# Pairing the low-rank passes of a fused cross-attention and FFN kernel in 64-row halves, with the group loop written out

## What is computed

```python
# cross-attention: layernorm, q/k/v projections, softmax over 256 keys, output projection
x = x + xattn(layernorm(x), ctx_768, ...)
# FFN with ternary weights and a low-rank term
def bitlinear(x, w):                      # w is rounded to -1, 0, 1 times a scale per row
    scale = clip(mean(abs(w), axis=1, keepdims=True), 1e-05, None)
    return x @ (clip(round(w / scale), -1.0, 1.0) * scale).T
n = layernorm(x)
h = bitlinear(n, w_fc) + gate * (n @ v.T @ fast_b.T @ u.T)     # rank 16
r = maximum(h, 0.0)
x = x + bitlinear(r * r, w_proj)
```

## Time and profile before

| what | value |
|---|---|
| median of three runs | 883.82 us (883.44 to 884.13) |
| profiled execution, first to last instruction | 881.4 us |
| profiled execution, its own time beside the span | not given; the median is 2.4 us above the span |
| mean granted TensorE clock | 0.972 |
| TensorE matmul busy | 831.4 us, 4104 instructions |
| VectorE busy | 581.0 us, 1142 instructions |
| ScalarE busy | 325.4 us, 632 instructions |
| GpSimd busy | 175.6 us, 156 instructions |
| matmuls of L1152, L1134, L1158 | 1024, 1008, 128 |

### The profile page before, as it was taken

One profiled execution on the slowest core, in us unless ns is written; L12 is line 12 of the kernel. 1 busy time (PEld: TensorE's weight loads), 2 busy tenths in 40 slices (PEclk: granted clock), 3 DMA queues, 4 the chain that ended last, 5 costly groups with the idle time before them and its releaser, 6 DMA issues.

```text
span 881.4 us, 12019 instructions
## 1 busy us (share of the span) xinstructions
PE 831.4 (94%) x4104; PEld 683.9 (78%) x4104; DVE 581.0 (66%) x1142; ACT 325.4 (37%) x632; POOL 175.6 (20%) x156
## 2 busy tenths in 40 slices
PE   5598778999999999999999999999999999999997
PEld 3365566888888888888788888887888888888885
DVE  4879758647783678557674778367755777477434
ACT  3364612434243423442343424342244233342432
POOL 1644514001240015002220124001500132012101
PEclk9879878999999999999999999999999999999999
DMA  9623110101011101110110101110110010000101
GB/s 329 145 84 108 49 37 0 48 1 36 1 52 45 36 1 48 48 37 1 51 49 1 36 1 51 45 37 2 49 48 25 13 48 1 1 1 1 49 0 48
DMA packets 19522, 36.66 MB, mean 42 GB/s; under 512 B 6898, under 2 KB 6898, under 8 KB 19460
## 3 DMA queue, kind: packets, MB, share of 16 engines
q1 hardware_dynamic: 18004, 35.84, 12.0%
q10 hardware_dynamic: 1456, 0.01, 0.1%
HBM read 27.45 MB, written 8.39 MB: 41 GB/s over the span
## 4 chain that ended last, share of the span: by engine, by line
PE 88%; DVE 8%; issue 2%; ACT 1%; DMA 1%; POOL 0%; SPq 0%; DVEq 0%; ACTq 0%; POOLq 0%
PE H L1152 27%; PE O L1134 26%; PE G L1052 23%; PE H L1158 3%; PE G L1078 3%; DVE above L950 1%; DVE below L951 1%; PE H L1052 1%; PE H L1028 1%; PE G L1107 1%; PE H L1078 1%; PE H L1016 1%; PE H L1036 1%; DMA Wq_s<-in_L_xattn_Wq_dram 1%; DVE n1T L857 0%
## 5 line engine op out<-in xcount | busy, mean ns | idle before, releaser
L1152 PE MATMUL H<-xnT,fcT 128*128 128x512 f32 x1024 | 258.1, 394 | 0.0
L1134 PE MATMUL O<-projT,qbuf 128*128 128x512 f32 x1008 | 253.3, 393 | 3.3 <-issue 3.3
L1134 PEld LDWEIGHTS O<-projT,qbuf 128*128 128x128 f32 x1008 | 186.3, 188 | 40.9 <-issue 3.7
L1152 PEld LDWEIGHTS H<-xnT,fcT 128*128 128x128 f32 x1024 | 189.1, 189 | 37.2
L685 ACT ACTIVATE qbuf<-rbuf 128x512 fp32r<-128x512 f32 x128 | 80.8, 631 | 161.2 <-DVE rbuf L926 93.4
L926 DVE TENSOR_TENSOR rbuf<-rbuf 128x512 f32<-128x512 f32 x128 | 105.5, 824 | 39.9 <-ACT rbuf L679 39.0
L930 DVE TENSOR_TENSOR qbuf<-rbuf,qbuf 128x512 fp32r<-128x512 f32 x128 | 97.0, 758 | 50.1 <-ACT qbuf L685 49.9
L679 ACT ACTIVATE rbuf<-H,scf 128x512 f32<-128x512 f32 x128 | 87.2, 681 | 89.3 <-PE H L1158 89.3
L564 POOL TENSOR_TENSOR xrs<-xrs,mhalf 128x4 f32<-128x4 f32 x9 | 9.2, 1021 | 361.9 <-DVE xrs L892 361.9
L1052 PE MATMUL G<-n1T,M 128*128 128x512 f32 x276 | 65.5, 395 | 0.1
L1052 PE MATMUL G<-Wvo,tT 128*128 128x512 f32 x270 | 63.9, 389 | 1.5 <-DVE tT L812 1.5
(11 more groups left out here) (156 smaller groups left out, 989.7 us busy)
## 6 DMA issues: line engine op xcount, KB each, us to landing
xb<-in_x_dram SPq DMA_DIRECT2D x8, 1024.0 KB
ctxb<-in_ctx_dram SPq DMA_DIRECT2D x8, 768.0 KB
wring<-in_L_ffn_w_fc_dram SPq DMA_DIRECT2D x16, 256.0 KB, 5.7
wring<-in_L_ffn_w_proj_dram SPq DMA_DIRECT2D x16, 256.0 KB, 2.4
out_dram<-x2a SPq DMA_DIRECT2D x8, 512.0 KB, 2.6
out_dram<-x2b SPq DMA_DIRECT2D x6, 512.0 KB, 2.6
Wq_s<-in_L_xattn_Wq_dram SPq DMA_DIRECT2D x4, 256.0 KB, 4.2
Wo_s<-in_L_xattn_Wo_dram SPq DMA_DIRECT2D x1, 1024.0 KB, 15.7
```

Of the source, the lines that this page charges most:

```text
L1134: mm = pe.matmul(banks[f"O{t}"][:, :], qbuf[:, j % 2, h, t * P:(t + 1) * P], projT[:, j, :], start=(j == 0 and h == HI), stop=(j == NFF - ...
L1152: pe.matmul(banks[f"H{j % 2}"][:, :], fcT[:, k, j * P:(j + 1) * P], xnT[:, h, k, :], start=(k == 0 and h == HI), stop=False)
```

## The change

The stack of the low-rank term is cut from 128 to 64 rows: per half, four blocks of 16 rows, of which u's part is rounded, remainder, rounded, rounded, and the other side is rounded, rounded, its own remainder, and the remainder of FB. The product of two remainders is dropped. Both halves of 128 rows (rows 0 to 63, rows 64 to 127) hold the same. Two FFN blocks, j even and j + 1, take their low-rank passes one directly behind the other, behind block j's eight matmuls: the first on rows 0 to 63 into H0, closing block j's sum, the second on rows 64 to 127 into H1, opening block j + 1's sum, which its eight matmuls then add to and the last one closes. Before the pair, for j of 2 and more, TensorE waits for the ReLU of block j - 1. The subtraction L799, one instruction on 64 rows, becomes two on 16 rows each. The evacuation of FB on ScalarE and on VectorE becomes two instructions each; uprep makes 6 copies and 2 subtractions. The loop over bodies 1 to 6 and the sync engine's loop are written out.

```diff
             steps(-1, prologue_steps(engine))
             steps(0, body_steps(True, False, engine))
-            with e.Fori(0, (NG - 2) // 2) as pair:
-                for odd in (1, 0):
-                    steps(2 * pair + 2 - odd, body_steps(True, True, engine), odd)
+            for b in range(1, NG - 1):
+                steps(b, body_steps(True, True, engine))
             steps(NG - 1, body_steps(False, True, engine))
...
-        FBp = FB[:, :, :].rearrange("p k (a h n) -> p k a h n", a=2, h=2)
-
-        def fb_of(bank):
-            return bank[:, 0:KD * 64].rearrange("p (k a n) -> p k a n", k=KD, a=2)
+        FBp = FB[:, :, :].rearrange("p k (a m) -> p k a m", a=2)
+        LOWS = slice(3 * RK, 4 * RK)
+
+        def fb_whole(bank):
+            return bank[:, 0:KD * 64].rearrange("p (k m) -> p k m", k=KD)
...
-            with sp.Fori(0, 2) as pair:
-                for odd in (1, 0):
-                    store(2 * pair + 1 - odd, 1 - odd)
-                    load_next(2 * pair + 2 - odd)
+            for g in range(4):
+                store(g, g % 2)
+                load_next(g + 1)
...
-                    nc.scalar.activation(FBp[:, :, :, HI, :], fb_of(bank), ACT.Copy).then_inc(job_act, 1)
+                    for a in range(2):
+                        last = nc.scalar.activation(FBp[:, :, a, :], fb_whole(bank), ACT.Copy)
+                    last.then_inc(job_act, 1)
...
-                    nc.vector.tensor_tensor(FBp[:, :, :, LO, :], fb_of(bank), FBp[:, :, :, HI, :], ALU.subtract
-                                            ).then_inc(job_dve, 1)
+                    for a in range(2):
+                        last = nc.vector.tensor_tensor(FBp[:, :, a, LOWS], fb_whole(bank)[:, :, LOWS],
+                                                       FBp[:, :, a, LOWS], ALU.subtract)
+                    last.then_inc(job_dve, 1)
...
                 elif kind == "L":
-                    nc.vector.tensor_tensor(tstack[64:128, :], bank[64:128, :], tstack[64:128, :], ALU.subtract
-                                            ).then_inc(unit_dve, 1)
+                    for at in (2 * RK, 6 * RK):
+                        rows = slice(at, at + RK)
+                        last = nc.vector.tensor_tensor(tstack[rows, :], bank[rows, :], tstack[rows, :], ALU.subtract)
+                    last.then_inc(unit_dve, 1)
...
-                        for i in range(4):
-                            nc.vector.tensor_copy(unat[:, :, 2 * i, :], uhi[:, :, :])
-                            last = nc.vector.tensor_tensor(unat[:, :, 2 * i + 1, :], u_s[:, :, :], uhi[:, :, :],
+                        for a in range(2):
+                            for i in (0, 2, 3):
+                                nc.vector.tensor_copy(unat[:, :, 4 * a + i, :], uhi[:, :, :])
+                            last = nc.vector.tensor_tensor(unat[:, :, 4 * a + 1, :], u_s[:, :, :], uhi[:, :, :],
                                                            ALU.subtract)
...
                             for h in (HI, LO):
-                                pe.matmul(banks[f"H{j % 2}"][:, :], fcT[:, k, j * P:(j + 1) * P], xnT[:, h, k, :],
-                                          start=(k == 0 and h == HI), stop=False)
-                        if j == 0:
-                            pe.wait_ge(unit_dve, n_dve(b, ("L", 0)))
-                            if isinstance(b, int) and b == 0:
-                                pe.wait_ge(ut_stored, 4)
-                        pe.matmul(banks[f"H{j % 2}"][:, :], uT[:, j * P:(j + 1) * P], tstack[:, :],
-                                  start=False, stop=True).then_inc(up_full, 1)
+                                mm = pe.matmul(banks[f"H{j % 2}"][:, :], fcT[:, k, j * P:(j + 1) * P], xnT[:, h, k, :],
+                                               start=(j % 2 == 0 and k == 0 and h == HI),
+                                               stop=(j % 2 == 1 and k == KD - 1 and h == LO))
+                        if j % 2 == 1:
+                            mm.then_inc(up_full, 1)
+                        else:
+                            if j == 0:
+                                pe.wait_ge(unit_dve, n_dve(b, ("L", 0)))
+                                if isinstance(b, int) and b == 0:
+                                    pe.wait_ge(ut_stored, 4)
+                            else:
+                                pe.wait_ge(relu_made, NFF * b + j)
+                            pe.matmul(banks["H0"][:, :], uT[0:64, j * P:(j + 1) * P], tstack[0:64, :],
+                                      start=False, stop=True).then_inc(up_full, 1)
+                            pe.matmul(banks["H1"][:, :], uT[64:128, (j + 1) * P:(j + 2) * P], tstack[64:128, :],
+                                      start=True, stop=False)
```

## The result

The changed kernel takes 894.70 us, median of four runs (894.50 to 895.26), against 883.98 for the kernel before on the same chip: ratio 1.0123, 95% interval 1.0107 to 1.0139. It is slower by 10.7 us; 896 was predicted. Its profiled execution spans 892.7 us, 11.3 more than before.

What follows compares the result with a forecast made beforehand. TensorE's issued work was taken as the bound, busy 94% of the span. Terms -5.0 + 4.0 + 13.1 = +12.1 us on the 881.4 span, plus 2.4 for launch and end, gave 896 us; 8-in-10 range 868 to 904.

Steps and rivals of the forecast that it cites:

- Part 1: Group loop written out: two jumps back, 2.48 us each, disappear; -5.0 us, bounds 0 and -5.0.
- Part 2: Low-rank evacuation split in two on VectorE: the second instruction takes 0.60 us more, with no slack; +4.0 us, bounds 3 and 5.
- Part 3: Low-rank passes paired on row halves: 684 ns a pair against 454 for the two passes removed; +13.1 us in all.
- s: Cost of one change between full-array and half-array work, paid twice a pair: 0.20 us, bounds 0 and 0.20.
- The single row behind "fb": After the 16-row job "fb", full-array transposes' weight load comes 0.20 us after the last matmul starts, against 0.11 within the job.
- o: How much later a pair's second half starts: 0.06 us, between 0 and 0.11; 0.227 without overlap.
- Block 0: In 8 pairs TensorE already waits for VectorE's split subtraction, so one shape change is already paid; 30 ns remain, not 230.
- The faster rival: Pair halves run together and changes of shape are free: 868 us, chance 0.20.
- The new wait: Before a pair, TensorE waits for the previous block's ReLU to free bank H1; claimed covered, no charge.

Runs made afterwards that it cites:

- solo passes: Against the kernel before: loop written out, 64-row stack, one subtraction, every block its own unpaired low-rank pass on rows 0 to 63; 927.48 us, ratio 1.0497.
- On the same half: Changed kernel with the second pass of each pair also reading rows 0 to 63; 908.47 us, ratio 1.0291 to the kernel before.

## Why the prediction was right

The time was forecast at 896 and is 894.7, and it came out in the way described: two stops gone, a later subtraction, and pairs that overlap but pay for two changes of shape. The parts, by the bodies:

| term | forecast | measured, for 8 bodies |
|---|---|---|
| loop written out | -5.0 | -5.0 for the two jumps; +0.3 in straight bodies |
| split subtraction | +4.0 | 8 x 0.59 = +4.7 alone |
| order and new wait of the pairs | 0 | 8 x 0.09 = +0.7 |
| pairs on halves, less what block 0 waits for anyway | +13.1 | 8 x (96.73 - 95.34 - 0.09) = +10.4 |
| sum | +12.1 | +11.1; the median says +10.7, the spans +11.3 |

Where both edits meet, at block 0, some 0.20 us a body is paid once for the two. The forecast took it off the pairs, and so does the table. Taken off the subtraction instead, the same bodies give +3.1 (96.73 against 96.34) and 8 x (96.34 - 94.84) = +12.0, and the same sum.

That the sum is so close is in part luck: the pairs were put 2.7 us too high, the subtraction, the order and the loop together 1.7 too low. Pairs and subtraction each lie within the range given for them, and the errors offset each other.

- **Part 1** was right, and shown on both kernels. Writing out moved the stop nowhere; that bodies without the loop are a little longer (0.06 us in the kernel before, 0.13 in the changed one) was not foreseen and is not explained.
- **Part 2** was right in mechanism, its size 0.7 too small and inside its bounds of 3 and 5. (Its own terms, 7 x 0.47 + 0.60, make 3.9 and not 4.0.) The second instruction takes 0.71 us and not 0.60, because I took the pair time from two instructions on the same rows, and these work on different strips. The Trainium skill has this, in "VectorE: DVE Perf Modes", "Two Vector instructions with no wait between them": an instruction whose operands start in another quadrant of 32 partitions is held until the earlier ones have finished. The trace agrees: 1.40 against 1.29 us.
- **Part 3**, s: 0.20 forecast, 0.195 measured by the solo passes, and both its halves stand in the trace: 0.32 - 0.23 = 0.09 before the load, and 0.11 of load laid bare. The single row behind "fb" carried it, on 16 rows as on 64. The profile names the gap "issue", as it names the stop at the loop's jump; that label alone would not have told what it was. (The range of the forecast begins at 886 and not 887: s of 0.15 and o of 0 make this part 56 x 0.073 - 8 x 0.077 = +3.5.)
- **Part 3**, o: 0.06 forecast, under 0.01 measured, and this is the size that made the part too high: 64 x 0.057 is 3.6 us. It is the one term that I had no row for and split down the middle. With it at 0 a pair costs 0.86 - 0.23 = 0.63 us, 0.18 more than the two passes before.
- **Block 0**: I took 0.20 a body off, since TensorE stands waiting there. The runs show this credit: the subtraction costs 0.59 a body alone and 0.39 beside the pairs.
- **From the span to the time** I added 2.4 us as launch and end. In the changed kernel's executions the time lies 1.8 us above the span (894.51 and 892.7), so 0.6 of it was something else.
- **The faster rival** had half of its condition met. The halves start together: both records stand at 248.74, in agreement with the 4 ns of the Trainium skill, "TensorE: Matmul & The Clock Gate", Part 3. That s would be near 0 did not follow from it. The page has loads pulled ahead where their row groups don't conflict with the running ones, or into a background weight buffer; a full-array matmul runs on all rows, so the first can't be meant at the entry of a pair, and the second did not come about there: the load for the half stands at 248.74, with its matmul. The rival needed o + 2s under 0.21 us and got 0.40.
- **The new wait** did not show: the first half passes idle only behind VectorE (2.6 us in all, in the group's line above). The small price of the pair order, 0.09 us a body, is under what the times tell, and I have not looked for its cause.

## What to carry to other kernels

Passes on half the rows are worth it only in runs: one entry and one exit cost 0.40 us together here, nearly two whole passes of 512 columns, while pairing saves one pass. With a single pair between full-array matmuls that is a loss; several pairs behind one another would be needed to earn it back, which was not tried here. Before reshaping a few instructions, look in the trace for any place where the shape already changes and read the distance of starts there. And count VectorE instructions, not rows, where TensorE waits with no slack: by itself, cutting one subtraction in two cost 4.0 us, nearly all of the 4.3 that the unrolled loop had brought.

## What I had not expected

The loads of the two halves cost no more than one. Both load records of a pair stand at 248.74, and both matmuls last 0.50, each with 0.11 us of bare load in it: they loaded at the same time. The price agrees: a pair costs 0.63 us and a lone pass on half the rows 0.23 + 0.39 = 0.62. I had given the second load up to 0.11 us of its own. On the same half, by contrast, the second load hides under the first pass (0.39 and not 0.50), so loads are hidden inside the half-array shape and only at its borders laid bare.
